# A cross-attention layer: the attention weights are turned through DRAM and by VectorE instead of by TensorE

## What is computed

```
Q = x @ Wq;  K = ctx @ Wk;  V = ctx @ Wv            # per head
attn = softmax(Q @ K.T / sqrt(512), masked)          # 8 heads x 77 keys = 616 per row
out = concat_h(attn @ V) @ Wo + x
out = (out - mean) * rsqrt(var + 1e-5) * gamma + beta
```

## Time and profile before

| what | value |
|---|---|
| time, median of 3 runs | 354.24 us (353.8 to 354.63) |
| span of the profiled execution | 352.2 us; its own time is not given apart |
| TensorE busy | 346.3 us, 98% |
| VectorE busy | 285.9 us, 81% |
| ScalarE busy | 243.3 us, 69% |
| GpSimd busy | 213.2 us, 61% |
| DMA | 55.81 MB, mean 158 GB/s |

### The profile page before, as it was taken

One profiled execution on the slowest core, in us unless ns is written; L12 is line 12 of the kernel. 1 busy time (PEld: TensorE's weight loads), 2 busy tenths in 40 slices (PEclk: granted clock), 3 DMA queues, 4 the chain that ended last, 5 costly groups with the idle time before them and its releaser, 6 DMA issues.

```text
span 352.2 us, 6867 instructions
## 1 busy us (share of the span) xinstructions
PE 346.3 (98%) x2272; PEld 322.7 (92%) x2272; DVE 285.9 (81%) x523; ACT 243.3 (69%) x796; POOL 213.2 (61%) x218
## 2 busy tenths in 40 slices
PE   8999999999999999999999999999999999999994
PEld 6999999999999999998899899889988998999884
DVE  0159999999778767898798888987987989889896
ACT  3267766545777679887886976977778769768460
POOL 0045654400447958689769678688696696884243
PEclk9999999999999999999999999999999999999999
DMA  7998669775644080043152341440532413413012
GB/s 234 428 416 334 265 222 337 288 259 211 220 152 198 0 292 11 1 179 125 57 179 64 118 151 60 152 147 36 180 105 75 162 71 129 149 47 105 32 50 100
DMA packets 19683, 55.81 MB, mean 158 GB/s; under 512 B 1728, under 2 KB 3264, under 8 KB 17728
## 3 DMA queue, kind: packets, MB, share of 16 engines
q1 hardware_dynamic: 18784, 54.38, 42.8%
q10 hardware_dynamic: 864, 1.00, 1.0%
HBM read 46.98 MB, written 8.39 MB: 157 GB/s over the span
## 4 chain that ended last, share of the span: by engine, by line
PE 97%; DMA 1%; DVE 0%; DVEq 0%; issue 0%
PE pair L681 30%; PE pair L606 27%; PE pair L489 20%; PE pair L496 13%; PE pair L668 5%; PE pair L596 1%; PE pair L698 1%; DMA w_proj<-wk 1%; DVE centred L1199 0%; DVEq L105 0%; DVE stats_last L1191 0%; DVE mean_var L1196 0%; DVE var_eps L1171 0%; PE pair L616 0%; DVE out_sb L1185 0%
## 5 line engine op out<-in xcount | busy, mean ns | idle before, releaser
L1373 POOL TENSOR_TENSOR w_proj_lo<-w_proj,w_proj_hi 128x768 fp32r<-128x768 f32 x20 | 36.6, 1850 | 73.0 <-ACT w_proj_hi L766 73.0
L681 PE MATMUL pair<-vw_hi,pt_hi 128*128 128x512 f32 x155 | 62.3, 402 | 0.0
L681 PE MATMUL pair<-vw_hi,pt_lo 128*128 128x512 f32 x155 | 60.8, 392 | 0.0
L681 PE MATMUL pair<-vw_lo,pt_hi 128*128 128x512 f32 x155 | 60.6, 391 | 0.0
L1322 POOL TENSOR_TENSOR out_sb<-centred,beta_sb 128x512 f32<-128x512 f32 x30 | 38.9, 1296 | 28.9 <-ACT centred L875 28.8
L830 ACT ACTIVATE prob<-c,neg_max 128x77 f32<-128x77 f32 x128 | 44.0, 346 | 0.0
L489 PE MATMUL pair<-kv_t,w_out_hi 128*128 128x308 f32 x160 | 41.7, 334 | 0.0
L1367 POOL TENSOR_TENSOR xo_lo<-x_sum,xo_hi 128x512 fp32r<-128x512 f32 x32 | 41.4, 1299 | 0.2 <-ACT xo_hi L854 0.2
L606 PE MATMUL pair<-a_hi,xo_hi 128*128 128x308 f32 x128 | 40.4, 315 | 0.0
L606 PE MATMUL pair<-a_hi,xo_lo 128*128 128x308 f32 x128 | 38.9, 304 | 0.0
L606 PE MATMUL pair<-a_lo,xo_hi 128*128 128x308 f32 x128 | 38.9, 304 | 0.0
(11 more groups left out here) (117 smaller groups left out, 1015.1 us busy)
## 6 DMA issues: line engine op xcount, KB each, us to landing
w_out<-wo SPq DMA_DIRECT2D x8, 1024.0 KB, 4.8
xt_in<-x_tiles SPq DMA_DIRECT2D x16, 512.0 KB, 4.1
x_in<-x_rows SPq DMA_DIRECT2D x16, 512.0 KB, 4.9
out<-out_sb SPq DMA_DIRECT2D x31, 256.0 KB, 2.2
w_out<-wq_t SPq DMA_DIRECT2D x7, 1024.0 KB, 8.0
w_proj<-wv SPq DMA_DIRECT2D x8, 768.0 KB, 4.9
w_proj<-wk SPq DMA_DIRECT2D x6, 768.0 KB, 9.7
w_out<-wq_t SPq DMA_DIRECT2D x2, 512.0 KB, 8.0
```

The lines of the kernel that those rows point to most:

```text
L681: mm = pe.matmul(ps_out[:, i % 2, 0:s.model], ps[:, j, :], v[:, j, b, :], start=(j == 0 and n == 0), stop=(j == s.key_t - 1 and n == len(p ...
L1373: pool.tensor_tensor(half_cols(w_proj_lo[u % W_RING], half), half_cols(w_proj_sb[u % W_RING], half), half_cols(w_proj_hi[u % 2], half).bit ...
```

## The change

Tiles 2 to 29 are no longer turned by TensorE. Their `prob` (padded from 616 to 640 columns) goes to a DRAM tensor `shelf` in two DMAs (`shelve`), and comes back in four (`take_back`) to an SBUF tile `turned`, in which row blocks and column blocks of 32 have changed places: partition 32c + q holds rows 32r + q, columns of block c. VectorE's transpose turns each 32x32 block in place (`turn`, two instructions per tile, to `pt_blocks` in PSUM). `shelf` has two buffers, `turned` one, so `take_back` waits until the tile before has been turned. Tiles 0, 1, 30 and 31 stay with TensorE.

So that the pieces in DRAM are long, the keys are dealt out anew to the five key tiles: every third key of the first 384, every second of the other 256 (`key_tile`; `parts()` is ((0, 3), (3, 2)), `QUAD` is 32). A row's piece is 96 or 64 floats when written, 160 when read. Hence `vw`'s transposes read with a step, and they are planned later: three key tiles after heads 5, 6 and 7, and two (four groups of four transposes, one group before) in `first_products(0)`. GpSimd and VectorE clear the padding.

VectorE's `residual` stays for tiles 0 and 1 only. From tile 2 on, ScalarE copies x into the bank of `ps_out` ahead of `out_rows` (`x_out`), and the matmuls add to it. On VectorE `split_pt` moves: `turn` takes its place, and it follows after `moments`, or after `normalise(a)`.

```
+            plan[s.heads - first + j] = [(j, b) for b in range(s.batches)]
+    plan[s.heads] = [(j, b) for b in range(s.batches) for j in range(first, s.key_t)]
...
+        def key_tile(t, j):
+            first, count = s.parts()[j >= s.parts()[1][0]]
+            return t[:, first * P + j - first:(first + count) * P:count]
+        def by_dma(i):
+            return CHUNK <= i < T - CHUNK
...
             def load_x(c):
-                if c >= X_RING:
-                    sp.wait_ge(dve_resid, CHUNK * (c - X_RING + 1))
+                if c == X_RING:
+                    sp.wait_ge(dve_resid, CHUNK)
+                elif c > X_RING:
+                    sp.wait_ge(act_x_out, x_out_no(CHUNK * (c - X_RING + 1) - 1))
...
+            def shelve(i):
+                n = dma_before(i)
+                sp.wait_ge(dve_prob, i + 1)
+                for first, count in s.parts():
+                    sp.dma_start(shelf[n % 2][:, :, first * QUAD:(first + count) * QUAD],
+                                 prob[i % 2][:, first * P:(first + count) * P].rearrange("p (c n) -> p c n", c=P // QUAD))\
+                      .then_inc(shelved[n % 2], DMA_INC)
+
+            def take_back(i):
+                n = dma_before(i)
+                sp.wait_ge(shelved[n % 2], 2 * use(n, 2))
+                if n > 0:
+                    sp.wait_ge(dve_turned, 2 * n)
+                by_quad = shelf[n % 2].rearrange("(r q) c n -> c q r n", q=QUAD)
+                for c in range(P // QUAD):
+                    sp.dma_start(turned[c * QUAD:(c + 1) * QUAD, :, :], by_quad[c]).then_inc(back, DMA_INC)
...
                 t = i - OUT_RING
+                if by_dma(i):
+                    shelve(i)
+                    if i % 2:
+                        take_back(i)
...
+                if by_dma(i) and i % 2 == 0:
+                    take_back(i)
...
@@ TensorE, over pairs
                 first_products(p)
-                transpose_prob(a - 2)
                 out_rows(a - 3)
-                transpose_prob(a - 1)
                 product_s3(p)
...
@@ TensorE, out_rows
-                if i >= 2:
-                    pe.wait_ge(dve_centred, i - 1)
+                if i < 2:
+                    pe.wait_ge(dve_vw_lo, early + 3 + i)
+                else:
+                    pe.wait_ge(act_x_out, x_out_no(i))
...
@@ ScalarE
+            def x_out(i):
+                c = i // CHUNK
+                act.wait_ge(ld_x[c % X_RING], use(c, X_RING))
+                act.wait_ge(dve_centred, i - 1)
+                act.activation(ps_out[:, i % 2, 0:s.model], x_in[c % X_RING][:, i % CHUNK, :], ACT.Copy)\
+                   .then_inc(act_x_out, 1)
...
                 copy_s1(p)
-                split_pt(a - 2)
                 if p > 2:
+                    x_out(a - 2)
                     scale(a - 4)
...
+                split_pt(a - 2)
+                exps_first(p)
+                x_out(a - 1)
                 split_pt(a - 1)
-                exps_first(p)
                 scale(a - 3)
                 exps_second(p)
...
@@ VectorE
+            def turn(i):
+                dve.wait_ge(back, DMA_INC * (P // QUAD) * dma_before(i + 1))
+                dve.wait_ge(dve_pt_lo, i)
+                for first, count in s.parts():
+                    blocks = pt_blocks[:, first:first + count, :].rearrange("p j (r q) -> p r j q", q=QUAD)
+                    rows = turned[:, :, first * QUAD:(first + count) * QUAD].rearrange("p r (q j) -> p r j q", j=count)
+                    dve.transpose(blocks, rows).then_inc(dve_turned, 1)
...
                     normalise(a - 1)
-                    split_pt(a - 2)
-                residual(a - 3)
+                turn(a - 2)
+                if p == 2:
+                    residual(1)
                 moments(a - 3)
+                split_pt(a - 2)
                 combine_c22(p)
                 max_c11(p)
                 centre(a - 3, ps_out[:, (a - 3) % 2, 0:s.model])
                 combine_c12(p)
-                split_pt(a - 1)
+                turn(a - 1)
                 combine_c21(p)
                 normalise(a)
-                residual(a - 2)
+                split_pt(a - 1)
                 moments(a - 2)
```

More of the change, by code:

```diff
@@ L60, in __init__, with parts @@
         assert 2 * self.toks <= BANK and self.model <= BANK and self.dim_t == self.model_t == 4
-        assert self.batches == 2
-    def key_rows(self, j):
-        return min(P, self.row - j * P)
+        assert self.batches == 2 and self.key_t == 5
+    def parts(self):
+        return ((0, 3), (3, 2))
 def transposes_during(s):
[L70 to L76, removed]
+    plan = [[] for _ in range(s.heads + 1)]
+    (_, first), _ = s.parts()
+    for j in range(first):
+        plan[s.heads - first + j] = [(j, b) for b in range(s.batches)]
+    assert (s.heads - first) * s.keys >= first * P
+    plan[s.heads] = [(j, b) for b in range(s.batches) for j in range(first, s.key_t)]
     return plan
@@ L103, in build @@
     group_no = {g: n for n, g in enumerate(groups)}
+    early = sum(len(part) for part in plan[:H])
     with ExitStack() as stack:
@@ L181, in build @@
         c12 = sb("c12", [P, s.half])
-        sb("gap2", [P, 288])
-        prob1 = sb("prob1", [P, s.row])
+        prob1 = sb("prob1", [P, s.padded])
         neg_max = [sb(f"neg_max{n}", [P, H]) for n in range(2)]
@@ L212, in build @@
         stats_last = sb("stats_last", [P, 2, 6])
+        shelf = [nc.dram_tensor(f"shelf{n}", [P, P // QUAD, s.key_t * QUAD], F32, kind="Internal")
+                 for n in range(2)]
         pairs = [stack.enter_context(nc.psum_tensor(f"pair{n}", [P, 2, 512], F32)) for n in range(4)]
@@ L263, in build @@
         dve_centred, dve_pad, dve_last = sem("dve_centred"), sem("dve_pad"), sem("dve_last")
+        shelved = [sem(f"shelved{n}") for n in range(2)]
+        back, dve_turned = sem("back"), sem("dve_turned")
         pool_const, pool_p_lo = sem("pool_const"), sem("pool_p_lo")
@@ L295, in head_cols, with dma_before, pe_before, x_out_no @@
             return t[:, 2 * half:2 * half + 2, :, h * s.keys:(h + 1) * s.keys]
+        def key_tile(t, j):
[3 more added lines that the diff above has]
+            return CHUNK <= i < T - CHUNK
+        def dma_before(i):
+            return sum(by_dma(t) for t in range(i))
+        def pe_before(i):
+            return i - dma_before(i)
+        def x_out_no(i):
+            return i - CHUNK + 1
         def tile_cols(w, m):
@@ L595, in transpose_vw @@
                     for m in range(s.model_t):
-                        mm = pe.transpose(ps_vw(h, b)[0:rows, m * P:(m + 1) * P],
-                                          vw_t[:, m, b, j * P:j * P + rows], identity[:, :])
+                        mm = pe.transpose(ps_vw(j, b)[:, m * P:(m + 1) * P], key_tile(vw_t[:, m, b, :], j),
+                                          identity[:, :])
                     mm.then_inc(pe_vw, 1)
@@ L681, in out_rows @@
                         mm = pe.matmul(ps_out[:, i % 2, 0:s.model], ps[:, j, :], v[:, j, b, :],
-                                       start=(j == 0 and n == 0),
-                                       stop=(j == s.key_t - 1 and n == len(passes) - 1))
+                                       start=(i < CHUNK and j == 0 and n == 0),
+                                       stop=(j == s.key_t - 1 and n == len(passes) - 1),
+                                       skip_group_check=i >= CHUNK)
                 mm.then_inc(pe_out, 1)
@@ L730, in _ @@
             last_products(1)
-            pe.wait_ge(dve_vw_lo, len(groups))
             out_rows(0)
@@ L948, in _ @@
             last_x()
+            x_out(T - 2)
             scale(T - 4)
@@ L1290, in _ @@
                 centre(a - 2, ps_out[:, (a - 2) % 2, 0:s.model])
-            residual(T - 3)
             layer_norm(T - 3)
             split_pt(T - 1)
-            residual(T - 2)
             layer_norm(T - 2)
```

94 lines of the change are left out of this document (50 added, 44 removed).

## The result

The changed kernel takes 381.88 us (median of 4 runs, 379.98 to 383.75) against 354.33 us (353.8 to 354.63): a ratio of 1.078, 95% interval 1.074 to 1.083. It is 27.5 us slower. The forecast was 371.5, in a range of 350 to 398.

What follows compares the result with a forecast made beforehand. TensorE (98% busy) bounds the kernel before; after, the DRAM trip in series with VectorE's order. Time: 141.5 + 0.6 start + 14 x 15.05 period + 16.7 tail + 2.0 around the span = 371.5 us, range 350 to 398.

Steps and rivals of the forecast that it cites:

- The trip in series: One trip through DRAM per pair, the even tile's, counts in full in VectorE's order; forecast 6.9 us.
- R: Round trip through DRAM, from VectorE having normalised a tile until `turn` may start: 6.9 us, bounds 5.2 and 10.5.
- P = R + 2T + 6.43 + 0.1: Period of a tile pair: round trip, two `turn`s, VectorE's other work 4.18 + 2.25, ScalarE's later copies 0.1; 15.05 us.
- T: VectorE's `turn` of one tile, two instructions of 384 and 256 columns: 0.81 us, at most 1.6.
- The write's own sum: Write of `prob` to DRAM: wake-up 0.1, first byte 0.8, transfer 1.9, landing 0.5, together 3.3 us.
- rival (4): VectorE's `turn` costs twice as much, 1.6 us per tile: period 16.65, 394 us; chance 0.10.
- The odd tile's trip: Runs beside VectorE's work; its reads, 3.6 us, just fit under 4.2 us after the even `turn`.
- Small pieces: Transfer of the write's 64 pieces per DMA engine: 1.9 us, geometric middle of 0.9 (by bytes) and 4.2 (65 ns each).
- The floor: With 1.10 us of transposes off TensorE per pair, TensorE alone would allow a period of 12.80 us.
- Rival (1): The trip fits, little or no wait at `turn`: round trip under 5.7 us; chance 0.13 faster, 0.04 the same.
- SP's queue: Twelve more issues per pair at 0.45 us, 5.4 us in all, fit in SP's waiting time; delay 0.
- Rivals (3): Small pieces are dear, 65 ns each: round trip 9.2 us, 404 us, or milder 8.3 and 391; chance 0.13.

Runs made afterwards that it cites:

- e1: Changed kernel without the DRAM transfers: VectorE's transpose reads `prob` itself, so the block exchange is left out; 352.9 us.
- e2: Changed kernel with one write of whole `prob` rows in place of two writes of small pieces, same bytes, wrong layout for the reads; 372.9 us.
- e9: e8 with SP's four reads of a tile moved ahead of the loads and the store, directly behind the next tile's writes; 352.4 us.
- e6: Changed kernel, transfers kept, with ScalarE's copy of S1 for the next pair moved in between the second exponentials of the pair before; 378.7 us.
- e5: e1 with ScalarE's copy of S1 for the next pair moved in between the second exponentials of the pair before; 348.9 us.
- e4: Kernel before the change with only ScalarE's `x_out` in place of VectorE's `residual` from tile 2 on, transposes staying on TensorE; 355.7 us.
- e8: Changed kernel with `turn` and all that follows it one tile later, and ScalarE's copy of S1 moved early as in e6; 379.6 us.
- e10: e9 with two buffers for `turned`, a semaphore for each, and both sets of reads ahead of the stores in SP's order; 351.2 us.

## Why the prediction was right

The direction and the mechanism were right, and most terms stand near their forecasts; that the write does is partly luck. Of the signs named beforehand, TensorE was busy for 193.88 of the 218.16 us of the 14 pairs (89%, under the 93%), the larger wait was the even tile's, and a DMA of `turned` ended it.

- **The trip in series.** Forecast R = 6.9 (write 3.3, reads 3.6); measured 7.08 on average over 14 pairs (6.5 to 8.1), 3.50 and 3.57 for the halves. e1 shows that the trip carries the loss, e2 that 0.59 us of R moves P by 0.54, e9 that the time comes back once the trip is covered. The first form of the forecast, P = R + 2T + 6.43 + 0.1, gives 7.08 + 1.90 + 6.43 + 0.1 = 15.51 with the measured R and T; the period was 15.58.
- **The write's own sum.** The forecast was 0.8 to the first byte, 1.9 of transfer and 0.5 to the landing. The write issued at 241.97 shows otherwise (slices of 0.1 us from 242.0):

```profile
GB/s 147 199 198 160 141 109 64 0 0 0 0 54 253 269 242 261 253 253 256 231 295 197 205 224 213 103 18 18 15 0 0 0 0 0 0 0 0 0 0 0
```

Its bytes begin to move at 243.1, 1.1 us after issue, and end at about 244.55, after some 1.45 us; the reads are issued 0.9 us later. So the transfer was 0.45 us shorter than forecast, and the rest, which the forecast took from the row of a single plain store, was 0.7 us longer. The two errors nearly cancel.
- **T.** Forecast 0.81, measured 0.95 to the next start (the median of 28; 243.06 to 244.00 above). By shape:

```profile
L1212 DVE STREAM_TRANSPOSE pair<-turned 128x384 f32<-128x384 f32 x28 | 20.0, 713 | 27.1 <-DMA turned<-shelf 27.1
L1212 DVE STREAM_TRANSPOSE pair<-turned 128x256 f32<-128x256 f32 x28 | 11.7, 419 | 0.0
```

The narrow one took 0.42 us, exactly as priced from the earlier trace rows; the wide one 0.71 where 0.55 was priced, and the whole excess is there. It differs from the narrow one in width and in reading every third element instead of every second; no run separates the two. Both stay far from the 1.6 of rival (4). The two `turn`s add 0.28 us per pair, 3.9 us in all.
- **The odd tile's trip.** "They just fit" was nearly so: it was late in 5 of 14 pairs; its `turn` started 0.16 us after the end of the instruction ahead on average, where it starts 0.08 before that end when nothing is late. This takes the place of the 0.1 for ScalarE's later copies. With the averages of after, R 7.08, the even `turn` 0.99, from the next start to the end of the instruction ahead of the odd `turn` 4.17 (4.12 in the pair shown), the gap 0.16, the odd `turn` 0.95, and from the next start to the end of `normalise` 2.23: together 15.58, the period.
- **Idle time before the even `turn`.** Forecast 2.3, measured 1.72 on average: in the stretch ahead of it VectorE also waits for TensorE (0.47 us ahead of `moments` at 237.69) and ahead of `combine_first` (0.48 us at 239.94, no releaser named). Such waits lie in the shadow of the trip, as e6 showed.
- **Small pieces.** 1.9 us was a middle between 0.9 and 4.2, and the least supported term; the engines were busy for 1.30 us, some 20 ns a packet. The 65 ns of the upper bound were no price "whatever their size": those 864 packets held 1.00 MB, 1.2 KB each on average. The Trainium skill ("DMA: Bandwidth & Descriptors", Specifications) says that pieces under 512 B are read-modify-written and miss line rate. That they miss it agrees: e2's pieces of 2560 bytes took 0.84 us for the same bytes. Taken as a doubling, as the prediction tried, the rule would have made R 8.8 and the time some 398 us; 28 x 1024 = 28,672 pieces of 256 and 384 bytes were written, and R is 7.08. Whether a read-modify-write takes place, no run shows.
- **The floor.** Here the prediction was wrong, though it hardly bore on the forecast. TensorE alone was to allow 12.80. With no trip the period was 13.6 (e1), with one copy moved 13.2 steady (e5), and TensorE itself was busy for 12.93 us of that. I had read VectorE's load (12.4) and ScalarE's (12.2) singly, "under any P below"; in e1 the order in which they wait for one another bounds first. Rival (1) would at a hidden trip have brought 353 us, not 340.
- **`x_out` and the tail.** Kept at 16.7, measured 17.9; e4 shows 1.0 of the 1.1 us with `x_out` alone.
- **The start.** Forecast 0.6, measured 0.7, but this confirms nothing: `normalise(2)` ended anywhere from 141.3 (e8) to 142.3 (after) in kernels with the same start, and at 142.2 in e4, which has the old one.
- **SP's queue.** For the even tile 0 was right at the change's own order: its reads were issued at least 1.0 us after the store ahead of them. An issue of a write takes 0.60 us and not 0.45. The odd tile's writes were held up by 0.4 us on average, at most 1.5, as they stand behind the issuing of the even tile's reads. e8 shows what the same queue costs in another order.

From 371.5 to 381.9: R 14 x 0.18 = 2.5, T 3.9, the odd trip and the rest of P 14 x 0.07 = 1.0, start and tail 1.2, scatter around the span 1.6; together 10.2 of 10.4 us.

Rivals (3) and (4) are refuted by R and T: the one needed R of 8.3 to 9.2, the other T of 1.6; the 20 ns a packet speaks against (3) directly. Rival (1) failed by its own number: R had to be under 5.7.

Open: why the wide transpose is dear; how much of e2's 0.75 us in the write is the spared issue, beside the 0.46 of the pieces; whether issues from another engine's queue would shorten the trip; and whether a tail in the old order would give e10 its lost 5 us. None was tried.

## What to carry to other kernels

The price of sending this work through DRAM was the latency from the last producer to the first consumer (7 us for 320 KB each way, in six DMAs), not the bytes or the engine time. Elsewhere, count first what the in-order consumer has to do between the two. If it is less, add distance before anything else is tuned, and then read the DMA queue in its own order: a transfer behind one that waits for somebody else loses the whole gain (e8 and e9 differ in the place of one step and by 27 us). Only then do small edits in the loop pay in full (e5 against e6).

## What the runs showed of the hardware

VectorE's transpose of 32x32 blocks of fp32, SBUF to PSUM, took 713 ns for 384 columns read with a step of three elements and 419 ns for 256 columns with a step of two, 0.95 us for both in a row. A write of 256- and 384-byte pieces to DRAM kept each DMA engine busy for 1.30 us per 320 KB, one of 2560-byte pieces for 0.84. An issue on SP of a write in 512 pieces took 0.60 us (1.21 for two), one of a write in 128 rows of 640 floats 0.34.

TensorE's clock fell where TensorE had stood. One stretch of after, in slices of 1 us (columns as in the earlier trace rows):

```profile
182.00:183.00 1.00, 0.00 (x0) 0.00 (x0) 0.97 (x3) 0.70 (x1) 0.76 (x1) 1.00 0.21 53
...
186.00:187.00 1.00, 1.00 (x4) 0.83 (x3) 1.00 (x3) 0.97 (x6) 0.00 (x0) 0.50 0.74 225
...
192.00:193.00 1.00, 1.00 (x9) 1.00 (x8) 0.93 (x4) 0.72 (x4) 0.00 (x0) 1.00 0.68 250
```

and the matmul that ended the idle stretch:

```profile
184.49 0.59 PE L662 MATMUL pair<-t_hi,xo_hi 128*128 128x308 f32 x1 [3.70 <-DVE c L1165]
```

TensorE had idled 3.7 us. The granted clock was then 0.50 of full, 1.2 GHz, until after 190, with 4 matmuls per us against 9 later. This is how a kernel with 140 matmuls less is busy for longer. The period, though, is accounted for above without it, by VectorE's chain of waits and work. In e8, where VectorE waits for its reads for 2.4 us per pair, the mean clock was 0.993 against 0.964 in after, and the period 15.30: a late read stretches the period with the clock nearly whole, too. No run changes the clock alone, so that it adds nothing in after is argued and not shown.
